# A four-block graph network on one core: where the two halves of an aggregated sum and the self term are added in blocks 1 and 2

## The reference

```python
x = layernorm(x + gat(x, adj, W_stack))            # two attention layers
x = layernorm(x + relu(A_norm @ x @ W))            # block 1: A_norm = D^-1/2 (A + I) D^-1/2
x = layernorm(x + relu((A / deg) @ x @ W_neigh.T + b_neigh + x @ W_self.T + b_self))   # block 2
x = layernorm(x + (A @ (relu(A @ (x @ W1) + b1) @ W2) + b2))    # block 3, two sums over A
```

## Time and profile before

| | |
|---|---|
| median of 3 runs | 762.22 us (759.72 to 762.22) |
| the profiled execution | 764.73 us, of which its span is 762.9 us |
| granted clock of TensorE, mean | 0.994 |
| TensorE matmuls busy | 728.3 us, 95% of the span |
| VectorE busy | 479.6 us, 63% |
| ScalarE busy | 351.3 us, 46% |
| GpSimd busy | 345.2 us, 45% |
| aggregation stages | from about 510 us to the end; block 1 to about 601 us, block 2 to about 675 us |

### The profile page before, as it was taken

How to read it: one execution, slowest core, us unless ns; L and a number is a source line. 1 busy time by engine, 2 the same in 40 slices (tenths; PEclk the granted TensorE clock), 3 DMA queues, 4 the chain that set the end, 5 groups by cost and what they waited for, 6 DMA issues and landing times.

```text
span 762.9 us, 13840 instructions
## 1 busy us (share of the span) xinstructions
PE 728.3 (95%) x4074; PEld 619.1 (81%) x4074; DVE 479.6 (63%) x1110; ACT 351.3 (46%) x832; POOL 345.2 (45%) x377
## 2 busy tenths in 40 slices
PE   6979999999999998999999999989999999999995
PEld 5868888888888887888888888877768776789884
DVE  2566777777777655655756656564687656753465
ACT  3665656565666455365465555531222322322221
POOL 1045767677676415555454454565672011113231
PEclk9999999999999999999999999999999999999998
DMA  6043242423332201532231322364752223320032
GB/s 206 1 165 139 84 165 84 152 96 130 118 112 107 99 28 57 147 129 70 90 116 69 128 78 76 105 128 112 187 148 73 83 64 98 91 68 1 21 98 92
DMA packets 67749, 76.61 MB, mean 100 GB/s; under 512 B 36848, under 2 KB 61040, under 8 KB 63600
## 3 DMA queue, kind: packets, MB, share of 16 engines
q1 hardware_dynamic: 67696, 75.97, 31.6%
HBM read 48.69 MB, written 18.87 MB: 89 GB/s over the span
## 4 chain that ended last, share of the span: by engine, by line
PE 84%; DVE 6%; ACT 3%; issue 3%; DMA 2%; POOL 2%; SPq 0%; DVEq 0%; ACTq 0%; POOLq 0%
PE scores L1764 37%; PE ob L1764 26%; PE tb L1764 9%; PE tb L1892 7%; PE xb L1764 1%; POOL prob L644 1%; PE tb L1868 1%; DVE xt_l L1153 1%; ACT sd L1006 1%; DVE zb L1558 1%; ACT xt_h L739 1%; DVE xs L1590 1%; DVE norm_values L1564 1%; DMA rin<-self_term_scratch 1%; DMA keep<-in_x 1%
## 5 line engine op out<-in xcount | busy, mean ns | idle before, releaser
L644 POOL TENSOR_TENSOR prob<-prob,arow 128x512 f32<-128x512 f32 x128 | 193.1, 1531 | 160.3 <-ACT prob L839 160.3
L1764 PE MATMUL ob<-val,stationary 128*128 128x512 f32 x960 | 186.6, 344 | 0.0
L1764 PEld LDWEIGHTS ob<-val,stationary 128*128 128x128 f32 x960 | 146.7, 189 | 18.4
L1153 DVE TENSOR_TENSOR stationary<-tb,stationary 128x512 fp32r<-128x512 f32 x128 | 85.6, 688 | 60.0 <-ACT stationary L739 58.8
L1764 PE MATMUL scores<-wst_h,whs_h 128*128 128x512 f32 x256 | 103.6, 405 | 4.0 <-ACT prob L839 4.0
L1764 PE MATMUL scores<-wst_l,whs_h 128*128 128x512 f32 x256 | 100.5, 393 | 0.0
L1764 PE MATMUL scores<-wst_h,whs_l 128*128 128x512 f32 x256 | 100.5, 393 | 0.0
L1258 DVE TENSOR_REDUCE row_values<-scores 128x1 f32<-128x512 f32 x128 | 86.0, 683 | 17.7 <-PE scores L1764 16.0
L739 ACT ACTIVATE stationary<-tb 128x512 fp32r<-128x512 f32 x128 | 73.0, 594 | 45.0 <-PE tb L1892 43.5
L839 ACT ACTIVATE prob<-scores,row_values 128x512 f32<-128x512 f32 x128 | 86.6, 689 | 4.9 <-DVE row_values L1265 4.9
L1764 PE MATMUL tb<-pm,adjr 128*128 128x512 f32 (+1 forms) x384 | 85.5, 362 | 0.0
(11 more groups left out here) (182 smaller groups left out, 1170.1 us busy)
## 6 DMA issues: line engine op xcount, KB each, us to landing
arow<-in_adj SPq DMA_DIRECT2D x32, 1024.0 KB, 5.1
adjacency_halves<-arow SPq DMA_DIRECT2D x16, 512.0 KB, 2.9
features_scratch<-xs SPq DMA_DIRECT2D x48, 128.0 KB, 1.8
xres<-features_scratch SPq DMA_DIRECT2D x48, 128.0 KB, 2.2
keep<-in_x SPq DMA_DIRECT2D x4, 512.0 KB, 6.4
xres<-in_x SPq DMA_DIRECT2D x16, 128.0 KB, 2.1
self_term_scratch<-rst SPq DMA_DIRECT2D x16, 128.0 KB, 1.7
rin<-self_term_scratch SPq DMA_DIRECT2D x16, 128.0 KB, 2.2
```

What stands on the lines that cost most here:

```text
L644: nc.gpsimd.tensor_tensor(prob[u][:, cs], prob[u][:, cs], arow[u][:, cs], ALU.mult).then_inc(g.msk.sem, 1)
L1153: return nc.vector.tensor_tensor(dst, v, h.bitcast(F32), ALU.subtract)
L1764: return nc.tensor.matmul(o, l, r, start=start, stop=stop)
```

## The change

In blocks 1 and 2 on the route `exact()`, VectorE makes the total with two instructions that both read PSUM: high sum times the scale plus `rin` into `zb`, then, after a wait for the first (`s_high`), low sum times the scale plus `zb` into `zb`, which posts `a.r`. It waits for the sums (`a.done`) itself. ScalarE's `lo_half` goes: in block 1 its place in the program is taken by `self_scaled`, which multiplies `rin` by `dinv` in place, from SBUF to SBUF; in block 2 nothing takes it. GpSimd's `term` of block 2 goes, and its signals are posted in one step. `self_loop` waits for `C.r` in place of `s_loop`, and SyncE's load of `rin` for `a.r` of the tile before last.

```diff
--- before.py
+++ after.py
@@ -356,7 +356,8 @@
         s_bt = sem("block3_biases_loaded")
         s_last = sem("block1_last_tile_chunks_done")
         s_self = sem("self_loops_ready")
-        s_loop = sem("self_loops_added")
+        s_loop = sem("self_loops_scaled")
+        s_high = sem("high_sums_added")
         s_part = sem("block3_moving_low_parts")
         s_emov = sem("block3_moving_ready")
 
@@ -506,6 +507,7 @@
                             ge(sp, a.y, t - 1)
                             sp.dma_start(xres[u][:, :], xs_rows[t]).then_inc(a.xres[u].sem, 16)
                         if a.load_self:
+                            ge(sp, a.r, t - 1)
                             sp.dma_start(rin[u][:, :], rs_rows[t]).then_inc(a.rin[u].sem, 16)
 
                     def store(b, u):
@@ -698,9 +700,12 @@
                     ge(pool, a.xres[u], 8 * b + 16)
                     nc.gpsimd.tensor_tensor(xres[u][:, :], xres[u][:, :], bout[:, :], ALU.add).then_inc(a.rb.sem, 1)
 
-            def terms():
+            def terms(quick):
                 pool.wait_ge(s_bt, 32)
-                for a in (Dg, E, F):
+                if quick:
+
+                    pool.sem_inc(Dg.rb.sem, NT)
+                for a in (E, F) if quick else (Dg, E, F):
                     with pool.Fori(0, NT // 2) as half:
                         b = 2 * half
                         term(a, b, 0)
@@ -710,12 +715,12 @@
 
                 pool.wait_ge(n_pl, NT)
                 pool.wait_ge(n_prj, NT)
-                ge(pool, s_loop, t - 1)
+                ge(pool, C.r, t - 1)
                 nc.gpsimd.tensor_tensor(rin[t % 2][:, :], pm[:, t, 0:D].bitcast(F32), pm[:, t, D:2 * D].bitcast(F32),
                                         ALU.add).then_inc(s_self, 1)
 
             def general():
-                terms()
+                terms(False)
 
             def exact():
                 for t in range(NT):
@@ -724,7 +729,7 @@
                         widen_next = t + RING - 1
                         if widen_next < NT:
                             widen(widen_next)
-                terms()
+                terms(True)
 
             pool.wait_ge(s_flag, 1)
             low = pool.value_load(anylow[0:1, 0:1])
@@ -1018,7 +1023,13 @@
                         else:
                             copy(keep[:, t, 0:width], jb[u][:, 0:width]).then_inc(a.pk.sem, 1)
 
-                return split, rows_hi, lo_half, deviation, keep_proj
+                def self_scaled(b, u):
+
+                    t = b + u
+                    act.wait_ge(s_self, t + 1)
+                    copy(rin[u][:, :], rin[u][:, :], scale=dinv[:, t:t + 1]).then_inc(s_loop, 1)
+
+                return split, rows_hi, lo_half, deviation, keep_proj, self_scaled
 
             def general():
 
@@ -1027,7 +1038,7 @@
                         keep_adj(q, c)
 
                 for k, a in enumerate(aggs):
-                    split, rows_hi, lo_half, deviation, keep_proj = parts(k, a, False)
+                    split, rows_hi, lo_half, deviation, keep_proj, _ = parts(k, a, False)
 
                     def hi(t, c):
                         n = 4 * t + c
@@ -1078,8 +1089,15 @@
             def exact():
 
                 for k, a in enumerate(aggs):
-                    _, rows_hi, lo_half, deviation, keep_proj = parts(k, a, True)
+                    _, rows_hi, lo_half, deviation, keep_proj, self_scaled = parts(k, a, True)
                     split = parts(k + 1, aggs[k + 1], True)[0] if not a.last else None
+                    if a is C:
+                        lo_half = self_scaled
+                    if a is Dg:
+                        act.sem_inc(E.tmp.sem, 2 * NT)
+
+                        def lo_half(b, u):
+                            pass
 
                     def slot(b, u, ep=True, fin=True):
                         p, pp = before(b, u), before(b, u, 2)
@@ -1495,9 +1513,28 @@
                         rest(xt_l[u][:, 0:kt, :], xb[u][:, 0:kt * P].rearrange("p (k i) -> p k i", k=kt),
                              xt_h[u][:, 0:kt, :]).then_inc(a.xtl.sem, 1)
 
+                def high_low(b, u):
+
+                    t = b + u
+                    scale = (dinv if a is C else rdeg)[:, t:t + 1]
+                    ge(dve, a.y, t - 1)
+                    if a is C:
+                        dve.wait_ge(s_loop, t + 1)
+                    else:
+                        ge(dve, a.rin[u], 8 * b + 16)
+                    dve.wait_ge(a.done, t + 1)
+                    nc.vector.scalar_tensor_tensor(zb[u][:, :], bank(b, u)[:, 0:w], scale, rin[u][:, :],
+                                                   ALU.mult, ALU.add).then_inc(s_high, 1)
+                    dve.wait_ge(s_high, NT * k + t + 1)
+                    nc.vector.scalar_tensor_tensor(zb[u][:, :], bank(b, u)[:, w:2 * w], scale, zb[u][:, :],
+                                                   ALU.mult, ALU.add).then_inc(a.r.sem, 1)
+
                 def total(b, u):
 
                     t = b + u
+                    if quick and a in (C, Dg):
+                        high_low(b, u)
+                        return
                     ge(dve, a.tmp, t + 1)
                     if quick and a is E:
                         ge(dve, a.new, t - 1)
@@ -1511,11 +1548,6 @@
                                                        ALU.mult, ALU.add).then_inc(a.r.sem, 1)
                     else:
                         nc.vector.tensor_tensor(dst, o, tmp[:, 0:w], ALU.add).then_inc(a.r.sem, 1)
-                    if quick and a is C:
-                        dve.wait_ge(s_self, t + 1)
-                        ge(dve, a.r, t + 1)
-                        nc.vector.scalar_tensor_tensor(zb[u][:, :], rin[u][:, :], dinv[:, bass.ds(t, 1)], zb[u][:, :],
-                                                       ALU.mult, ALU.add).then_inc(s_loop, 1)
 
                 def rows_free(b, u):
 
@@ -1537,9 +1569,7 @@
 
                 def with_residual(b, u):
                     t = b + u
-                    if a is C and quick:
-                        dve.wait_ge(s_loop, t + 1)
-                    elif a is C:
+                    if a is C or quick and a is Dg:
                         ge(dve, a.r, t + 1)
                     else:
                         ge(dve, a.rb, t + 1)
```

## The result

| | before | changed |
|---|---|---|
| median | 762.22 us (20 runs) | 759.62 us (20 runs) |
| profiled execution, and its span | 764.73 us, 762.9 us | 761.82 us, 760.0 us |
| PE, DVE, ACT, POOL busy | 728.3, 479.6, 351.3, 345.2 us | 729.0, 482.9, 345.1, 333.2 us |

The ratio of the times is 0.9967, 95% interval 0.9954 to 0.998: 2.5 us faster, between 1.5 and 3.5. The forecast was 1.2 us faster, 761.0 us; the direction was right, and the gain is twice as large. The prediction held a change of its size to be one that a measurement can't tell from none; with 20 runs each the interval leaves no change out, and it leaves the forecast 1.2 out too.

The account below looks back on a forecast made before the run. TensorE was taken as the bound (84% of the chain that ended last), with at most 5.9 us of waits to win. The terms -0.45, 0, -0.68, -0.2, 0, +0.13 and 0 gave -1.2 us: 761.0 us, range 757.5 to 763.8.

Parts of the forecast that it names:

- Step 1: First tile of block 1: VectorE starts 0.51 us sooner and TensorE's 0.45 wait for `xs` goes, -0.45 us.
- Step 2: Rest of block 1: VectorE keeps two instructions per tile, so 0, between -0.3 and +0.3 us.
- Step 4: Quick stretch of block 2: tile period falls from 4.06 to 3.98, second instruction 0.59 after the first, -0.2 us.
- Step 3: First tile of block 2: the relu starts 0.83 sooner and TensorE's wait for `xs` goes whole, -0.68 us.
- Step 5: Stretches of block 2 that TensorE sets: VectorE's free time covers its added work, 0.
- Step 6: End of block 2: `xt_l` of tile 14 stands behind one instruction more, +0.13 us.
- Step 7: Added waits (banks freed later, VectorE waiting for `rin`, SyncE's for a total): 0, up to +0.5 us.
- signs of being wrong: Quick stretches shrink over 1 us, PSUM instruction over 0.6, VectorE waits for `rin`, TensorE waits between 618 and 635 us.
- (c): Rival: VectorE becomes the bound in block 2 and the kernel slower, 770.2 us; chance 4%.
- (d): Rival: tiles wait for the transfer of the self term, 765.8 us; chance 2%.
- (b): Rival: all of TensorE's waits in blocks 1 and 2 go, 756.3 us, half of it 759.3; chance 11%.
- (a): Rival: time won at the head of a block is lost again in VectorE's stretch, 762.2 us; chance 17%.

Follow-up runs that it names:

- e1: Changed kernel with block 2's part undone, so only block 1 is changed: 761.67 us, ratio 0.9986 to the kernel before.
- e10: The changed kernel itself, measured again without any edit: 760.35 us, ratio 0.9973 to the kernel before.
- e9: Changed kernel with VectorE's `xt_l` of the tile before put between the two PSUM instructions, in both blocks: 761.66 us, ratio 0.9992 to the kernel before.
- e5: Changed kernel with SyncE issuing block 1's store of the self term ahead of the transposing load: 759.39 us, ratio 0.9955 to the kernel before.
- e7: Changed kernel, but block 2 keeps ScalarE's `tmp` and only GpSimd's step goes: 761.15 us, ratio 0.9985 to the kernel before.
- e8: Changed kernel plus a third VectorE instruction per tile of block 2, its result unused: 765.31 us, ratio 1.0031 to the kernel before.
- e2: Changed kernel with block 1's part undone, so only block 2 is changed: 760.08 us, ratio 0.998 to the kernel before.
- e3: Changed kernel with a second, already met wait ahead of the second PSUM instruction: 760.99 us, ratio 0.9996 to the kernel before.
- e4: Changed kernel with GpSimd's `self_loop` of block 1 let go after the relu instead of before: 763.66 us, ratio 1.0017 to the kernel before.

## Why the prediction was right, and where it was short

**Step 1** said -0.45 and was -0.60 (e1 -0.60), and -0.33 in e10. Two things were missed. The row of a TensorE wait leaves out about 0.15; and the first instruction starts either about 0.1 or about 0.4 us after the modelled end of the bank's last matmul, from one execution to the next, which no row of one profile could tell. Of the 11 executions with VectorE's new head three start early (changed, e1, e9) and eight late (one of them 0.5). What sets it stays open. With the late start the step is worth 0.29 to 0.33 where the edit leaves the head as it is (e5, e7, e8, e10), so the 0.60 of the first profile is the rarer case, and that -0.45 lies between the two is luck. The wait itself went whole, as said; in e7 0.2 us of it is left.

**Step 2** said 0 (-0.3 to +0.3) and was -0.22 to -0.33 in the quick stretch of block 1. The named reason for a gain, a relu that escapes GpSimd, came true: the relu fell from 12.2 to 9.5 us over the 16 tiles, in tiles 5 to 10 from 5.6 to 4.9. The step missed a second one, the shorter distance of step 4: between tiles 9 and 10, where the relu takes 0.94 in both, the period fell from 4.30 to 4.23. How the gain divides between the two isn't shown. The sentence that nothing here changes for the relu failed for tiles 5, 8 and 11 to 13. The size is steady: 27.22 to 27.37 in the five executions with this block 1 (changed, e10, e1, e7, e8), 27.55 and 27.66 in the two without. Of the two instructions, the longer PSUM read weighed against in the prediction doesn't exist: both take 0.48. By the 0.06 us per moved read of the Trainium skill (VectorE: DVE Perf Modes, "The TRN2 errata") line 1529 should have been longer than line 1517, an estimate of 0.54; the trace has 0.48 for both, and it is the trace that decides.

**Step 3** said -0.68 and was -0.85, the understated wait again, with the 0.51 to 0.52 distance behind it.

**Step 4** said -0.2 and was -0.44 (e2 the same). This is the term that was mis-sized by its working: the 0.59 was taken from a line with two waits (e3: 0.07 for the second). With 0.51 the period is 3.90, and it was 3.89; 3.98 had been forecast. The saving is 0.17 for each tile, not 0.08, and TensorE's waits for `xs` in this stretch went from 3.1 to 1.8 us. The sentence that the later `xt_l` "only fills that wait" was half right: TensorE waits 0.8 us for it here, which the shorter wait for `xs` more than pays for, and e9 shows that an earlier place would cost more.

TensorE's waits in this stretch, `xs` and `xt_l` together, come to 2.6 us, close to the 2.5 of the forecast, but it had put them all on `xs`.

**Step 5** held: 17.53 for 17.60, and with a third instruction still 17.60 (e8).

**Step 6** said +0.13 and was +0.18.

**Step 7** held: VectorE shows no wait for `rin`; the store of the self term kept it 0.9 us before and 0.8 after.

In sum the steps are -0.60, -0.33, -0.85, -0.44, +0.18, and -0.22 in the stretches between: -2.26, where the forecast had -1.2. With the late start of step 1 the sum would be some 0.3 smaller, as in e10. So the mechanism of steps 1, 3 and 4 was right, and their sizes were too small, each by a price that the rows before gave too high (0.59) or a wait that they gave too low. None of the signs of being wrong came; of the others, the distance of 0.59 and the `xt_l` that isn't waited for except at tile 14 failed. Of the signs that were named, VectorE's busy time rose by 3.3 us and not by 8: block 2's second instructions add 7.7 and the relu of block 1 gives back 2.7; of another 1.7 less, 0.3 is line 1517 in tile 1 (0.81, now 0.48), and the rest I didn't follow. GpSimd's fell by 12.0 (11.8 said), ScalarE's by 6.2 (8 said). Rivals (c) and (d) didn't come. (b) didn't either, since 4.9 us of waits are left, though the gain came out between the forecast and its half of 2.9. (a) is ruled out by e1's place in the table, though not by its time.

## What to carry to other kernels

When an engine is to take over a chain of small dependent steps, price the distance between starts and not the duration, and take it from a row with the same number of waits. Read the wait of TensorE as a lower bound, and compare positions of the same instruction in both traces to get the size. If a side engine's work is moved out of one instruction's way, look which one it falls on next, and what stands behind it in the DMA queue.

## What the runs showed of the hardware that was not expected

- An already met second wait in front of a dependent VectorE instruction costs 0.07 us (e3), and a third instruction between two dependent ones adds only 0.39 to a tile, less than the 0.48 that it takes: the one behind it, with no wait of its own left, starts 0.40 after it (e8).
- `xs`, with one input in SBUF, takes 0.79 beside GpSimd's widening and 0.41 alone (e4), but 0.50 beside it in tile 0 of the changed kernel; the relu, with two, takes 0.94 beside `self_loop` and 0.42 alone.
- After one wait of 2.12 us TensorE's granted clock was 0.57 over 4 us, so mostly the lower of its two levels, 1.2 GHz of 2.4 (e4).
- The stages ahead of block 1 vary, in part with the clock. The same 40 us in two executions of the changed kernel, e10's first:

```profile
20.00:60.00 40.00, 35.56 (x183) 29.40 (x182) 24.56 (x40) 23.00 (x47) 8.45 (x7) 0.96 0.28 106
```

```profile
20.00:60.00 40.00, 36.58 (x181) 30.15 (x181) 24.57 (x41) 23.09 (x47) 8.14 (x6) 0.91 0.28 105
```

TensorE is busy 1.02 us longer at 0.91 than at 0.96 for about as many instructions. The clock isn't all: the kernel before has 0.96 there too, and its fixed point lies 2.5 us behind e10's. Most of the spread is made in the first 60 us, where TensorE gets through 226 matmuls before, 234 in the changed kernel, 241 in e10 and 247 in e1, in the order of their fixed points (525.32, 524.70, 522.85, 521.79); why isn't shown. In the 20 runs of the changed kernel the median is 759.3 us for the 11 whose mean granted clock is 0.993 or more and 761.9 for the others. A change of this size is hard to see in that, unless it is measured from a point behind it.
